# Filler products for TensorE in a two-layer kernel ordered by a table

## The reference

```python
# layer 0
xn = layernorm(x)
q, k, v = xn @ Wq + bq, xn @ Wk + bk, xn @ Wv + bv            # 16 heads of 8, sequences of 256
attn = softmax(causal(q @ k.T / sqrt(8))) @ v @ Wm + bm
shared = silu(xn @ Sg) * (xn @ Su) @ Sd
routed = sum over the top 2 of 16 experts: p_e * (silu(xn @ Wg[e]) * (xn @ Wu[e]) @ Wd[e])   # width 64
x = x + attn + shared + routed
# layer 1
xn = layernorm(x)
q, k = l2norm(xn @ Wq), l2norm(xn @ Wk); v = xn @ Wv; b = sigmoid(xn @ Wbeta)
state_t = state_(t-1) * (1 - b k k^T elementwise) + b v k^T;   out_t = state_t q_t          # delta rule over time
attn = (layernorm(out) * ln_g + ln_b) * silu(xn @ Wg) @ Wout
routed = sum over the top 2 of 4 usable experts: w_e * (silu(xn @ w1[e]) * (xn @ w3[e]) @ w2[e])  # width 704
x = x + attn + routed
```

## Time and profile before

| | us |
|---|---|
| median of 3 runs | 1837.27 |
| lowest, highest | 1831.5, 1842.78 |
| profiled execution | 1826.7 |
| its span, first to last instruction | 1825.0 |
| mean granted clock of TensorE | 0.893 |

### The profile page before, as it was taken

The page is one execution under the profiler, slowest core; times in us unless marked ns, Lnnn a source line. Parts: engine busy times, 40 slices in busy tenths (PEclk is TensorE's granted clock), DMA queues, the critical chain, the costliest instruction groups (busy, mean ns, idle before and its releaser), DMA issues.

```text
span 1825.0 us, 32119 instructions
## 1 busy us (share of the span) xinstructions
PE 1484.2 (81%) x10982; PEld 1047.2 (57%) x10982; DVE 1394.5 (76%) x2664; ACT 955.9 (52%) x1562; POOL 921.8 (51%) x973
## 2 busy tenths in 40 slices
PE   3867887898878998788863999989999999999720
PEld 3733444455545554344432878867788777788520
DVE  6898765677667778767786688867888989998872
ACT  4724655566556565345653455555655555565520
POOL 5238766624655247667787016552122454662176
PEclk9868988999889898779986999999999999999955
DMA  8956898889886766466537556866565777775333
GB/s 273 281 149 183 234 249 238 262 233 268 211 248 200 195 165 179 115 163 179 147 100 248 161 189 202 252 170 197 157 193 162 231 220 223 215 246 161 90 87 95
DMA packets 277954, 354.58 MB, mean 194 GB/s; under 512 B 32272, under 2 KB 204304, under 8 KB 272416
## 3 DMA queue, kind: packets, MB, share of 16 engines
q1 hardware_dynamic: 237600, 287.92, 55.8%
q0 software_dynamic: 17056, 33.66, 6.4%
q10 hardware_dynamic: 23136, 30.94, 4.8%
HBM read 197.48 MB, written 122.68 MB: 175 GB/s over the span
## 4 chain that ended last, share of the span: by engine, by line
PE 45%; DVE 16%; POOL 11%; issue 10%; ACT 9%; another core or an unknown queue 3%; DMA 3%; SPq 2%; ACTq 1%; DVEq 0%; POOLq 0%
PE Y L1076 8%; PE R L832 6%; PE R L834 5%; PE R L833 5%; POOL xs_dram L1384 4%; POOL gat L1360 4%; PE R L935 3%; PE R L848 3%; PE Y L970 3%; DVE row_max L1933 2%; POOL o_acc L1404 2%; DVE state L2034 2%; ACT probs L1551 2%; PE R L955 2%
## 5 line engine op out<-in xcount | busy, mean ns | idle before, releaser
L1384 POOL DMA_INDIRECT xs_dram<-sc_in,pos x256 | 272.2, 1063 | 126.7 <-issue 57.0
L1404 POOL TENSOR_TENSOR o_acc<-o_acc,read 128x512 f32<-128x512 f32 x112 | 147.4, 1316 | 338.7 <-DVE read L2044 337.3
L1933 DVE TENSOR_REDUCE row_max<-R 128x6 f32<-128x768 f32 x256 | 240.2, 952 | 89.7 <-PE R L935 71.3
L1360 POOL DMA_INDIRECT gat<-ys_dram,pos x256 | 263.4, 1029 | 84.8 <-issue 59.0
L1395 POOL TENSOR_SCALAR_AFFINE_SELECT probs<-probs 128x512 f32<-128x512 f32 x256 | 169.6, 663 | 230.5 <-ACT probs L1551 224.0
L1551 ACT ACTIVATE probs<-R 128x768 f32<-128x768 f32 x256 | 204.8, 808 | 126.3 <-PE R L958 105.4
L1076 PEld LDWEIGHTS Y<-fd,hid 128*128 128x128 f32 (+1 forms) x1824 | 236.4, 193 | 50.3 <-DVE hid L2082 18.1
L1076 PE MATMUL Y<-fd,hid 128*128 128x128 f32 (+1 forms) x1824 | 250.5, 280 | 13.0 <-DVE hid L2082 10.6
L832 PE MATMUL R<-fhl,fw 128*128 128x512 f32 x418 | 182.8, 437 | 0.1
L2082 DVE TENSOR_TENSOR hid<-R,sil 128x512 f32<-128x512 f32 x228 | 156.3, 686 | 34.1 <-ACT sil L1670 18.8
L1670 ACT ACTIVATE sil<-R 128x512 f32<-128x512 f32 x190 | 112.6, 594 | 127.8 <-PE R L834 101.1
(11 more groups left out here) (267 smaller groups left out, 3322.3 us busy)
## 6 DMA issues: line engine op xcount, KB each, us to landing
fw<-wf SPq DMA_DIRECT2D x38, 1408.0 KB
q_rows<-kq SPq DMA_DIRECT2D x128, 256.0 KB, 5.4
fx<-xs_dram SPq DMA_DIRECT2D x86, 256.0 KB
xs_dram<-gat SPq DMA_DIRECT2D x24, 512.0 KB, 5.4
qk_dram<-qk_parts SPq DMA_DIRECT2D x32, 384.0 KB
Q<-qk_dram SPq DMA_DIRECT2D x64, 192.0 KB
K<-qk_dram SPq DMA_DIRECT2D x64, 192.0 KB
fw<-wf SPq DMA_DIRECT2D x96, 128.0 KB
```

The costliest lines, as they stand in the source:

```text
L1360: pool.indirect_dma_start(gat[:, i % 2, 2 * t + a, :], None, ys_dram[l][g], bass.IndirectOffsetOnAxis(ap=pos[l][g][a][:, col:col + 1], axi ...
L1384: pool.indirect_dma_start(xs_dram[g], bass.IndirectOffsetOnAxis(ap=pos[l][g][a][:, col:col + 1], axis=0), sc_in[:, n % 2, t * P:(t + 1) * ...
L1404: pool.tensor_tensor(o_acc[:, :], o_acc[:, :], read[:, j % 2, :], ALU.add)\
L1933: dve.tensor_reduce(row_max[:, b, h2, :, :], pair[:, :].rearrange("p (g c t) -> p g c t", g=2, t=P)[:, :, 0:3, :], AX.X, ALU.max).then_inc ...
```

## The change

In the play-through, from 20 us on, when TensorE is idle, no part of it can start, a bank of ring R is free and parts of it are still to come, a part FILL of 0.22 us is put into its order, on the bank that has been free longest. In the program FILL is one matmul of 512 bf16 columns, an identity against itself, whose result nobody reads. It waits for the release of the bank's last user and leaves the bank without a user. It signals nothing. Besides, nine ranks change. The diff, cut to its core:

```diff
+    FILLER, FILL_FROM = 0.22, 20.0
...
+        fillers, unfilled = [], sum(part[1] == "PE" for part in self.parts)
...
                 if i < 0:
+                    if i == -2:
+                        busy["PE"] = False
                     continue
...
                         events.append((now + self.parts[i][2], 1, i))
+                        unfilled -= e == "PE"
                         break
+                else:
+                    empty = [b for b, h in enumerate(held["R"]) if h is None]
+                    if e == "PE" and not busy[e] and unfilled and empty and now >= self.FILL_FROM:
+                        busy[e] = True
+                        fillers.append(("FILL", len(fillers), 0, min(empty, key=lambda b: since["R"][b])))
+                        result[e].append(fillers[-1][:3])
+                        events.append((now + self.FILLER, 1, -2))
...
+        places.update((filler[:3], [filler[3]]) for filler in fillers)
...
-        t = 221.9 + 51.5 * (n - 2)
+        t = 222.2 + 45.3 * (n - 2)
...
-    tb = a_time(NCH - 1) + 7.1
-    fast = 23
+    tb = a_time(NCH - 1) + 6.4
+    fast = 22
     def hw(j):
-        return tb + (20.9 * j if j < fast else 20.9 * fast + 21.5 * (j - fast))
+        return tb + (21.1 * j if j < fast else 21.1 * fast + 24.5 * (j - fast))
...
-    f0 = [f0_start + 8.8 * f - 59.0 * (f >= NT[0][0]) for f in range(sum(NT[0]))]
+    f0 = [f0_start + 8.1 * f - 54.5 * (f >= NT[0][0]) for f in range(sum(NT[0]))]
...
-        d.append(max(t, d[-1] + 37.8) if d else max(t, b_end - 60))
+        d.append(max(t, d[-1] + 37.6) if d else max(t, b_end - 60))
...
-            t = max(f1[sum(NT[1][:g + 1]) - 1] + 71.2, d[n] + 56, t + 10)
+            t = max(f1[sum(NT[1][:g + 1]) - 1] + 59.4, d[n] + 56, t + 10)
...
-    route(0, 0, a_time(7) + 21.1)
-    scatter(0, 0, a_time(7) + 62.9, 9.3)
+    route(0, 0, a_time(7) + 26.1)
+    scatter(0, 0, a_time(7) + 62.9, 8.8)
...
-    route(1, 0, c_end[0] + -27.5)
+    route(1, 0, c_end[0] + -26.7)
...
-    route(1, 1, c_end[1] + -27.5)
+    route(1, 1, c_end[1] + -26.7)
...
             for kind, n, k in ORDER["PE"]:
                 places = iter(BANKS[kind, n, k])
+                if kind == "FILL":
+                    if n == 0:
+                        pe.wait_ge(consts_v, CONSTS_V)
+                    b = next(places)
+                    if users["R"][b]:
+                        pe.wait_ge(*users["R"][b].released())
+                    users["R"][b] = None
+                    pe.matmul(psum["R"][:, b * C:(b + 1) * C], ident_b[:, :],
+                              ident_b[:, :].unsqueeze(1).to_broadcast([P, TILES, P]), start=True, stop=True)
```

More of the change, by code:

```diff
@@ L207, in order @@
                         events.append((now + self.parts[i][2], 1, i))
+                        unfilled -= e == "PE"
                         break
-        left = [name for i, name in enumerate(names) if missing[i]]
-        assert sum(map(len, result.values())) == len(names), left[:8]
-        return result, behind, {names[i][:3]: [chosen[i, j] for j in range(len(self.takes.get(i, ())))]
-                        for i in range(len(names)) if self.parts[i][1] == "PE"}
+                else:
[5 more added lines that the diff above has]
+                        events.append((now + self.FILLER, 1, -2))
+        left = [name for i, name in enumerate(names) if missing[i]]
+        assert sum(map(len, result.values())) == len(names) + len(fillers), left[:8]
+        places = {names[i][:3]: [chosen[i, j] for j in range(len(self.takes.get(i, ())))]
+                  for i in range(len(names)) if self.parts[i][1] == "PE"}
+        places.update((filler[:3], [filler[3]]) for filler in fillers)
+        return result, behind, places
 def table():
```

## The result

The changed kernel is slower: median 1848.4 us against 1835.4 for the kernel before (20 runs each), ratio 1.008, 95% interval 1.0056 to 1.0104. I had forecast 1809, in a range from 1775 to 1850: wrong in sign.

What follows compares the result with a forecast made beforehand. No engine fills the chain alone; TensorE has 45% of it, at a mean clock of 0.893. Clock 29 - product waits 9 + ranks 8 = 28 us gained, forecasting a median of 1809 us, range 1775 to 1850.

Steps and rivals of the forecast that it cites:

- Clock falls after thin stretches; the lower level costs 40%: TensorE, mixed stages: short thin windows drop the clock for the dense stretch behind; 0.40 of low-level time could be saved.
- Number of products: Filler matmuls on TensorE: 1,057 of 0.22 us, counted in 243 places of the old play-through.
- Products, net: 29 gained, 9 lost, so 20: Whole span: higher clock gains 29 us; parts waiting behind products cost 9, bounds 0 and 69.
- The rate 0.55: Whole span: share of TensorE's busy time on the chain, 821 of 1484 us, turning TensorE time saved into span.
- Ranks: 8 us gained: Seam between attention and large experts: scatters ahead of late masks and sums shorten it by at most 18 us, taken as 8.
- a rank decides only which ready part goes first: All engines' orders: a part with its inputs there starts whatever its rank, so most moved ranks count 0.
- the seam: Around 970 to 1000 us, last attention chunk to first large expert tile; TensorE busy 5.9 of 30 us; 8 us gained.
- This is a count, not a time on the chip: Caveat on the 1,057 products from the old play-through: new ranks will move the number; 1,057 taken anyway.
- The products stand in the way: Rival, 150 to 970 us: products stand before ready TensorE parts; 13 to 38 us slower, 1850 to 1875; chance 0.14.
- The signs I had named: Prediction wrong if clock up but first large tile as late, bank-release waits on new line, or large-expert stage grows over 14 us.
- Stage of the large experts: 38 tiles from 1000 to 1720 us: still 710 to 720 us, growing at most by its 64 products' 14 us.
- The Trainium skill's rule: Whole span: low-clock ramp costs under 1%, so gain under 10 us, too small to tell; supports "nothing happens", chance 0.18.

## Why the prediction was wrong, point by point

- **Clock falls after thin stretches; the lower level costs 40%:** right in part. With products the clock rose where they are dense, 0.84 to 0.95 from 700 to 970. From 150 to 700, where I had half of the low time removed, it stayed at 0.91 against before; only against the same order without products did it rise (0.84 to 0.91 on A). No run shows the 40% by itself.
- **Number of products:** 1,057 counted in the gaps of the old play-through. The change's own code puts 943 with the old ranks and 942 with the new, so the new ranks did not move the number. In the trace of the changed kernel there are 211 from 700 to 970 where I had 380 to the first large tile, 182 from 150 to 700 (188), 141 from 1000 to 1720 (64).
- **Products, net: 29 gained, 9 lost, so 20:** measured 24 (A) and 18 (B), with the order held fixed. That the size fits in the order that the change brings is luck: I had worked it out from rows of the order of before, and there it measures 2 us (A) and 4 (B; 8 by the medians) instead of 20. The rate 0.55, TensorE's share of the chain over its busy time, is the term I hold to have failed: it is a mean over stages. In the order of the old ranks the clock from 700 to 970 rose from 0.79 to 0.95 and the first large result moved by 0.8 us, so in these two profiles TensorE's time there was worth next to nothing. That the order of before has less to give because its engines fit each other closely is my reading; no run shows its mechanism.
- **Ranks: 8 us gained:** this is the step that failed, together with the order that the products draw when they are played, which I put at nothing. The ranks alone measure +41 us (A: 1875.2 - 1834.0) and +42 us (B: 1811.2 - 1769.1). The change's whole order, ranks and played products, none issued, measures +38 (A) and +42 (B). The played products alone, with the old ranks, measure +20 (A: 1855.1 - 1834.7) and +36 (B: 1806.6 - 1770.5). So either half redraws the order and loses, and the two don't add up. I reasoned over what each rank means, one at a time, from the closed formulas, and wrote "a rank decides only which ready part goes first" with 0 behind it for most. A greedy play-through is not smooth in its ranks: 0.1 us moves a fifth of TensorE's order and costs 1.7%. I had priced only the seam, and gave it the wrong sign: attention's end moved from 958.5 to 991.8. The same paragraph had its rank end 39 us later (795 to 834) and said that the seam then gains nothing; I took 8 all the same. That the ranks' meaning set the loss was my next theory, and it fell as well.
- **"This is a count, not a time on the chip":** I used the old play-through for counting gaps and did not ask what the products and ranks do to the order it yields. No rival held this. "The products stand in the way" has the right side, but not the mechanism: where they stood before ready parts, at the start, the most that could be seen was 9 us, and over the whole they gained.
- **The signs I had named:** the clock was up and the first large tile later than before, at 1019, not at 965 to 980: this sign of being wrong came. So did waits for a bank's release on the new line, but small: 7.9 us in 10 waits behind the first 25.3, the largest group 4.2 us in 4 for attn (L1986). TensorE's busy time rose by 168 us where I had 150.
- **Stage of the large experts:** 700.6 us from first to last result before, 712.0 after. I had bounded it by its products' 14 us and would have read the 11 as theirs. But without any product it is 713.8 (A), and with the old ranks and products 693.7: the order again.
- **The Trainium skill's rule** ("TensorE: Matmul & The Clock Gate", section "What's actually happening", not the one named in the prediction: the ramp penalty is under 1% of a typical kernel's span) gave a gain too small to tell. It speaks of one ramp; here the clock falls again and again, and my estimate of the loss was 4.8% of the span. The time in the order of before came out as by the rule, but not for its reason: the clock was low for about 0.21 of the span there.

What stays open: why products gain 1.0 to 1.3% in one order, 0.5% in a second and nothing measurable in that of before, with the clock raised in all three; which of the products gain; whether a new table costs by its order or by the banks of PSUM, which it assigns anew as well; and what lies behind the waits that only kind A has (last section).

## What to carry to other kernels

When work is ordered by a greedy list scheduler, every edit of it, also one that adds only filler or nudges a priority, is first a redraw of the whole order; compare it with the order held fixed (play the filler, don't issue it) before you judge the filler. Read the planner's own end time before and after: here it rose by 19 us (1637.1 to 1656.3), and all six tables whose end rose were slower on the chip. It is a warning, not a measure: the losses don't follow its size, and no table whose end fell was run. Filler that keeps TensorE's clock up was not worth a new order here: where it was played it gained 0.5 to 1.3% against the same order without it, and the new order had cost 1 to 2.5%. Put into a finished order it left the order alone, and its gain was too small to tell (three runs). A higher granted clock in the profile is no proof of a gain.

## What was not expected of the hardware

- The same program takes 3.3% less on one chip than on another: the change's order without products 1872.1 and 1810.9 us, though the busy times of VectorE, ScalarE and GpSimd agree within 0.3%; TensorE's is 1531.8 and 1485.6 us, at a granted clock of 0.865 and 0.897. In the profiles the last attention chunk is stored at 1016.7 and 950.5. What differs shows in the waits: on kind A some end at an event that no instruction or DMA of the profile explains ("remote"), as here, in the slower of the two (total us, times, longest):

```profile
ACT heads_out L1587 <- remote: 21.3, 7, 5.8
```

  All eight profiles of kind A have 28 to 41 such waits, 58 to 91 us in sum over the engines; in the kernel before they are 3.1% of the chain, 57 us. None of the twelve profiles of kind B has one. That they make most of the 64 us between the kinds (1834, 1770) is likely by their size and not shown, and what they are stays open. The ratio to the kernel before moves with the chip (1.0115 and 1.0248 for one kernel), so two kernels must be run on the same one.
- A matmul of 512 bf16 columns that nobody reads keeps the pace of 0.216 us at the full clock (17 in 3.83 us, the last with its modelled 0.38) and holds the clock at 1.00 through a stage in which TensorE had been idle for almost half the time at 0.60.
